# Scatters and gathers of 128 rows in place of 125, the last three to and from spare slots

## The chip, the cores and the metric

The kernel runs on one core of one Trainium2 chip. The metric is the device time of one execution in microseconds; its median of three runs is 7850.16 us. Engines are called by their names, and by the profile's short ones: TensorE (PE, with weight loads as PEld), VectorE (DVE), ScalarE (ACT), GpSimd (POOL), SyncE (SP). All of them issue work in program order and meet at semaphores. SyncE's DMAs go through queue 1, GpSimd's indirect ones through queue 0.

## The reference

Two layers of a graph transformer over 6250 nodes with 256 features. Only the last step of the second layer is touched: a mixture of eight experts, two for each node.

```python
x = x + _L1_ffn_ref(_layernorm(x), gate_w, gate_b, W1, b1, W2, b2)

# _L1_ffn_ref: N = 6250 rows, D = 256, H = 512, E = 8
logits = xf @ gate_w + gate_b
probs = softmax(logits)
top2_vals, top2_idx = top_k(probs, 2)
cw = zeros(N, E).at[rows, top2_idx].add(top2_vals)
for w1, bb1, w2, bb2, we in experts:
    h = gelu(xf @ w1 + bb1)
    out += we[:, None] * (h @ w2 + bb2)
```

## The kernel before

The 6250 rows stand in SBUF as NT = 50 tiles of P = 125 rows (`m.x`, 125 partitions x 50 x 256). `sorts_and_rows` sorts the edges and makes the rows' projections for the first layer, in an order of its engines' work that is written out once (`early_plan`, `weave`) and followed by each engine alone. Attention, slice attention and the relational layer follow, both graph layers with loops of indirect gathers of 128 rows (L1142 and L2055). The function `experts` comes last.

`experts` works in four steps.

1. *Gate.* ScalarE writes the normalized rows to `xn`, the first 125 partitions of the SBUF tensor `space` (128 x 50 x 256). TensorE turns each pair of tiles (L2760), VectorE copies the turned pair to SBUF (L2640), TensorE multiplies by the gate's weights (L2749), and VectorE and ScalarE make softmax and ranks in groups of GT = 10 tiles. TensorE and VectorE both wait for the gate's weights and bias (`s_g`) before their first work. At the end VectorE writes `place` (L2683): for each row and each of its two experts the slot in the sorted list.
2. *Scatter.* GpSimd issues 100 indirect DMAs (L2586), one for each tile and each choice, of 125 rows of 1 KB each, from `xn` to the DRAM tensor `moe_in`. It has MC = 105 chunks of 128 slots; each expert's rows begin at a chunk.
3. *Chunks.* SyncE waits for all scatters, loads `b1` and then the chunks (L2539) into a ring within `space`; TensorE, VectorE and ScalarE make the two products and the gelu; SyncE stores each chunk to `moe_out` (L2543).
4. *Gather.* After all stores GpSimd issues 100 indirect DMAs (L2595) that fetch each row's two results into a ring of RING_G = 8 slots, VectorE adds them with their weights to `m.x` (L2731, L2734), and SyncE stores five tiles at a time to the output (L2546).

Slots of `moe_in` that no row takes must hold finite numbers. SyncE fills the whole tensor with ones at L344, early in `sorts_and_rows`; the row stores of L365 and L366 stand behind it in the queue, and VectorE's copy at L607 waits for those stores before it may write its two row buffers again.

Of the kernel before, what the change touches and what calls it, by code (L numbers as in the profile page):

```python
# [13 lines left out]
ALU = mybir.AluOpType  # L14
ACT = mybir.ActivationFunctionType
AX = mybir.AxisListType
F32 = mybir.dt.float32
BF16 = mybir.dt.bfloat16
I32 = mybir.dt.int32
# [3 lines left out]
N, C, E = 6250, 256, 200000  # L23
P = 125
NT = N // P
H, D = 8, 32
EC = E // P
LANES = 128
# [187 lines left out]
def sorts_and_rows(nc, m, a, row_i, node_f):  # L216

    with ExitStack() as ctx:
        sb, ps, sem = m.scope(nc, ctx)
# [10 lines left out]
        s_fill, s_node_t, s_src = sem("se_s_fill"), sem("se_s_node_t"), sem("se_s_src")  # L230
# [39 lines left out]
        xn = [eb(f"xn{u}", [P, C]) for u in range(2)]  # L270
# [49 lines left out]
        with m.block() as block:  # L320
            @block.sync
            def _(sp):
                def sort_work():
                    sp.dma_start(key_a[:, :], a["src"].rearrange("(p j) -> p j", p=P)).then_inc(s_load, 16)
                    sp.dma_start(key_b[:, :], a["dst"].rearrange("(p j) -> p j", p=P)).then_inc(s_load, 16)
                    sp.dma_start(key_c[:, :], a["edge_type_8"].rearrange("(p j) -> p j", p=P)).then_inc(s_load, 16)
                    sp.dma_start(w_ps[:, :, 0:C], a["L0_gnn_Wp"].rearrange("(c p) n -> p c n", p=128)).then_inc(s_wp, 16)
                    sp.dma_start(w_ps[:, :, C:2 * C], a["L0_gnn_Wskip"].rearrange("(c p) n -> p c n", p=128)).then_inc(s_wp, 16)
                    sp.dma_start(w_kv[:, :, 0:C], a["L0_mix_Wk"].rearrange("(c p) n -> p c n", p=128)).then_inc(s_wp, 16)
                    sp.dma_start(w_kv[:, :, C:2 * C], a["L0_mix_Wv"].rearrange("(c p) n -> p c n", p=128)).then_inc(s_wp, 16)  # L330
                    sp.dma_start(a_row[:, 0, :], a["L0_gnn_a_src"].rearrange("a h f -> a (h f)").broadcast_to((128, C))).then_inc(s_wp, 16)
                    sp.dma_start(a_row[:, 1, :], a["L0_gnn_a_trg"].rearrange("a h f -> a (h f)").broadcast_to((128, C))).then_inc(s_wp, 16)
                    sp.dma_start(skip_b[:, :], a["L0_gnn_bias"].rearrange("(o c) -> o c", o=1)).then_inc(s_wp, 16)
                    sp.dma_start(w_q[:, :, :], a["L0_mix_Wq"].rearrange("(c p) n -> p c n", p=128)).then_inc(s_wq, 16)
                    sp.dma_start(w_m[:, :, :], a["L0_mix_Wm"].rearrange("(c p) n -> p c n", p=128)).then_inc(s_wq, 16)
                    sp.wait_ge(s_prep, 1)
                    sp.dma_start(key_c[:, :], a["dst"].rearrange("(p j) -> p j", p=P)).then_inc(s_load, 16)
                    sp.dma_start(key_b[:, :], a["src"].rearrange("(p j) -> p j", p=P)).then_inc(s_load, 16)
                    sp.dma_start(m.x[:, :, :], a["x"].rearrange("(t p) c -> p t c", p=P)).then_inc(s_x, 16)
                    for k in range(2 * COUNTED):  # L340
                        yield
                    sp.wait_ge(s_src, 1)
                    sp.dma_start(m.src_keys, keys[0][:, :]).then_inc(s_kept, 16)
                    sp.dma_start(m.moe_in.rearrange("(p a) (h c) -> p (a h) c", p=LANES, h=2),  # L344
                                 m.ones[:, :].unsqueeze(1).broadcast_to((128, 2 * MC, 128))).then_inc(s_fill, 16)
                    for k in range(SORTED):
                        yield

# [26 lines left out]
                sp.wait_ge(s_node_t, 1)  # L375
                sp.dma_start(m.node_t.rearrange("(p e) -> p e", p=128), keys[0][:, FS // 2:FS].bitcast(BF16)).then_inc(s_fill, 16)
                sp.wait_ge(s_kept, 16)
                sp.wait_ge(s_fill, 32)

            @block.vector  # L380
            def _(dve):
# [2069 lines left out]
GT = 10  # L2451
MC = (2 * N + NE * (LANES - 1)) // LANES
# [4 lines left out]
BACK_AT = HID_AT + 4  # L2457
RING_G = (NT - BACK_AT) // 2


def experts(nc, m, a, out):


    with ExitStack() as ctx:
        sb, ps, sem = m.scope(nc, ctx)
# [5 lines left out]
        space = sb("ex_space", [128, NT, C], F32)  # L2471
        xn = space[0:P, :, :]
        xs, ys = space[:, 0:RX, :], space[:, RX:RX + RY, :]
        b1 = space[:, BIAS_AT:HID_AT, :].rearrange("p (e h) c -> p e (h c)", h=2)
        hid = [space[:, HID_AT + 2 * u:HID_AT + 2 * u + 2, :].rearrange("p h c -> p (h c)") for u in range(2)]
        back = space[0:P, BACK_AT:BACK_AT + 2 * RING_G, :].rearrange("p (r k) c -> p r k c", k=2)
        xt = [sb(f"ex_xt{u}", [128, 2, 2 * P], F32) for u in range(2)]
        prob = sb("ex_prob", [P, NT, NE], F32)
        rank = sb("ex_rank", [P, NT, NE], F32)
# [10 lines left out]
        num = [sb(f"ex_num{u}", [P, NE], F32) for u in range(2)]  # L2490
        num_i = sb("ex_num_i", [P, NE], I32)
        base = sb("ex_base", [P, NE], F32)
        place = sb("ex_place", [P, 2, NT], I32)
        cw = sb("ex_cw", [P, 2, NT], F32)
        chunk_f = sb("ex_chunk_f", [1, MC], F32)
        chunk_e = sb("ex_chunk_e", [1, MC], I16)
# [12 lines left out]
                                     "s_sel", "s_pre", "s_place", "s_scat"))  # L2509
        s_b1, s_tc, s_xtc, s_h, s_hid, s_gelu, s_u, s_ht, s_y, s_ys, s_fin, s_out = (sem("ex_" + x) for x in (  # L2510
            "s_b1", "s_tc", "s_xtc", "s_h", "s_hid", "s_gelu", "s_u", "s_ht", "s_y", "s_ys", "s_fin", "s_out"))
        s_xs = [sem(f"ex_s_xs{r}") for r in range(RX)]
        s_st = [sem(f"ex_s_st{r}") for r in range(RY)]
        s_back = [sem(f"ex_s_back{r}") for r in range(RING_G)]
# [8 lines left out]
        with m.block() as block:  # L2523
# [26 lines left out]
            @block.scalar  # L2550
            def _(act):
                def exps(g):
                    act.wait_ge(s_sub, g + 1)
                    act.activation(prob[:, GT * g:GT * g + GT, :], prob[:, GT * g:GT * g + GT, :], ACT.Exp).then_inc(s_exp, 1)

                for i in range(pairs):
                    for j in range(2):
                        n = 2 * i + j
                        ins = act.activation(xn[:, n, :], m.x[:, n, :], ACT.Identity, scale=m.rstd[:, n:n + 1],
                                             bias=m.nmr[:, n:n + 1])  # L2560
                    ins.then_inc(s_xn, 1)
                    if i >= 7 and (i - 7) % 5 == 0:
                        exps((i - 7) // 5)
                exps(NT // GT - 1)
                for c in range(-2, MC - 1):
                    if c + 1 >= 0:
                        act.wait_ge(s_u, c + 2)
                        if c >= 1:
                            act.wait_ge(s_y, c)
                        act.copy(ht[(c + 1) % 2].rearrange("p q n -> p (q n)"), p_u[(c + 1) % 2][:, :]).then_inc(s_ht, 1)  # L2570
                    if c + 2 < MC:
                        act.wait_ge(s_hid, c + 3)
                        act.activation(hid[c % 2], hid[c % 2], ACT.Gelu).then_inc(s_gelu, 1)

            @block.gpsimd
            def _(pool):
                pool.affine_select(out=before[:, :, :], in_=m.ones[0:P, 0:NE * NE].rearrange("p (e j) -> p e j", e=NE),
                                   compare_op=ALU.is_gt, fill=0.0, base=0, pattern=[[1, NE], [-1, NE]],
                                   channel_multiplier=0).then_inc(s_tri, 1)
                pool.affine_select(out=tri_f[:, :], in_=m.ones[0:P, 0:P], compare_op=ALU.is_gt, fill=0.0, base=0,  # L2580
                                   pattern=[[1, P]], channel_multiplier=-1).then_inc(s_tri, 1)
                pool.wait_ge(s_xn, pairs)
                pool.wait_ge(s_place, 1)
                for n in range(NT):
                    for k in range(2):
                        pool.indirect_dma_start(out=m.moe_in, out_offset=bass.IndirectOffsetOnAxis(ap=place[:, k, n:n + 1], axis=0),  # L2586
                                                in_=xn[:, n, :], in_offset=None).then_inc(s_scat, 16)
                for r in range(RY):
                    pool.wait_ge(s_st[r], 16 * ((MC - 1 - r) // RY + 1))
                for n in range(NT):  # L2590
                    r = n % RING_G
                    if n >= RING_G:
                        pool.wait_ge(s_fin, n - RING_G + 1)
                    for k in range(2):
                        pool.indirect_dma_start(out=back[:, r, k, :], out_offset=None, in_=m.moe_out,  # L2595
                                                in_offset=bass.IndirectOffsetOnAxis(ap=place[:, k, n:n + 1], axis=0)
# [3 lines left out]
            def _(dve):  # L2600
# [28 lines left out]
                    dve.drain()  # L2629
                    dve.tensor_reduce(rank[:, GT * g:GT * g + GT, :], over[:, :, :, :], AX.X, ALU.add)  # L2630

                dve.wait_ge(s_tri, 2)
                dve.wait_ge(s_g, 32)
                dve.tensor_copy(tri[:, :], tri_f[:, :])
                dve.memset(full[:, :], 1.0)
# [17 lines left out]
                at, k = 0, 1  # L2653
# [26 lines left out]
                for k in range(2):  # L2680
                    dve.tensor_reduce(cw[:, k, :], run[k][:, :, :], AX.X, ALU.add)
                dve.drain()
                dve.tensor_copy(place[:, :, :], cw[:, :, :]).then_inc(s_place, 1)  # L2683
                dve.tensor_tensor(chunk_ge[:, :, :], m.count_p[0:1, 0:MC].unsqueeze(2).broadcast_to((1, MC, NE)),
                                  num[1][0:1, :].unsqueeze(1).broadcast_to((1, MC, NE)), ALU.is_ge)
                dve.drain()
# [19 lines left out]
                for c in range(-3, MC):  # L2706
                    if 0 <= c + 2 < MC:
                        k = c + 2
# [19 lines left out]
                for n in range(NT):  # L2728
                    r = n % RING_G
                    dve.wait_ge(s_back[r], 32 * (n // RING_G + 1))  # L2730
                    dve.scalar_tensor_tensor(out=back[:, r, 0, :], in0=back[:, r, 0, :], scalar=cw[:, 0, n:n + 1], in1=m.x[:, n, :],  # L2731
                                             op0=ALU.mult, op1=ALU.add)
                    dve.drain()
                    dve.scalar_tensor_tensor(out=m.x[:, n, :], in0=back[:, r, 1, :], scalar=cw[:, 1, n:n + 1],  # L2734
                                             in1=back[:, r, 0, :], op0=ALU.mult, op1=ALU.add).then_inc(s_fin, 1)

            @block.tensor
            def _(pe):
# [84 lines left out]
def program(nc, a, out):  # L2823
    with ExitStack() as ctx:
# [32 lines left out]
        m.skip_rows = nc.dram_tensor("skip_rows", (N, C), F32).ap()  # L2857
        m.table1 = nc.dram_tensor("table1", (R * N, C), F32).ap()
        m.node_t = nc.dram_tensor("node_t", (FS * LANES,), BF16).ap()
        m.moe_in = nc.dram_tensor("moe_in", (MC * LANES, C), F32).ap()  # L2860
        m.moe_out = nc.dram_tensor("moe_out", (MC * LANES, C), F32).ap()
        constants(nc, m)
        m.x = m.sb("x", [P, NT, C], F32)
        m.mean = m.sb("mean", [P, NT], F32)
# [102 lines left out]
```

## Time before and how its profile is read

| | |
|---|---|
| median of 3 runs | 7850.16 us (7850.01 to 7862.31) |
| the profiled execution | 7849.75 us |
| its span on the core | 7848.0 us |
| busy TensorE / VectorE / GpSimd | 69% / 66% / 44% of the span |

Busy times are sums over the instructions of an engine. The kernel is a row of stages with different limits, so a share of the whole span says little about one stage: stretches of the span are read instead. For a DMA that GpSimd issues, the duration in the trace is the engine's own work on it; when the data has landed is a second time, from issue to landing. "Idle before" is the time in which an engine did nothing ahead of an instruction, with what ended it; "issue" stands for nothing that the profile shows. "PEclk" is the granted TensorE clock as a share of its full speed.

### The profile page before, as it was taken

The numbers are of one execution on the slowest core, as the hardware profiler recorded it, in microseconds if no ns is written. First come the engines' busy times: TensorE is split into PE (matmuls) and PEld (weight loads), VectorE is DVE, ScalarE is ACT, GpSimd is POOL, SyncE is SP. The second block draws the span as 40 slices with busy tenths as digits, with TensorE's granted clock in tenths as the row PEclk, the third lists the DMA queues.
The fourth block names the chain that finished last, engine by engine and source line by source line (L and its number), as shares of the span: only waits on it lengthen the run. The fifth ranks groups of instructions, "written<-read, shape, count | busy, mean of one in ns | idle before, by whom it ended". The sixth has DMA issues, their size and how long they took to land. (4 is left out here: it accounts for less than half of the span.)

```text
span 7848.0 us, 86538 instructions
## 1 busy us (share of the span) xinstructions
PE 5431.4 (69%) x24766; PEld 3747.1 (48%) x24766; DVE 5164.8 (66%) x11681; ACT 1874.3 (24%) x4564; POOL 3485.0 (44%) x3441
## 2 busy tenths in 40 slices
PE   5877774555555555517799788888899999951991
PEld 2446663333333443314464333433777778750661
DVE  6457767888888877774467566676666767660332
ACT  0333332222223333212224200000222222210220
POOL 0000004777777777710000355555666777716006
PEclk8998886777777777759999899999999999965995
DMA  4100003444455555530013322222333333332223
GB/s 143 45 27 1 1 1 95 124 124 124 124 126 128 128 131 129 136 60 3 6 68 132 117 75 73 72 75 77 87 94 94 98 97 97 97 70 83 64 63 107
DMA packets 310188, 665.87 MB, mean 85 GB/s; under 512 B 77974, under 2 KB 173964, under 8 KB 302717
## 3 DMA queue, kind: packets, MB, share of 16 engines
q0 software_dynamic: 180352, 455.22, 23.0%
q1 hardware_dynamic: 129383, 205.31, 7.6%
q8 instruction: 199, 3.26, 0.2%
q14 instruction: 254, 2.08, 0.1%
HBM read 546.52 MB, written 113.55 MB: 84 GB/s over the span
## 5 line engine op out<-in xcount | busy, mean ns | idle before, releaser
L2055 POOL DMA_INDIRECT ag_rows<-table,row_src x1612 | 1595.8, 990 | 1896.5 <-POOLq L2847 1023.5
L1142 POOL DMA_INDIRECT at_rows<-table,row_dst x1612 | 1645.5, 1021 | 491.3 <-issue 450.8
L1308 PE MATMUL at_p_a<-at_rows,at_hot 128*125 128x264 f32 x3224 | 1132.0, 509 | 1014.6 <-issue 972.1
L1308 PEld LDWEIGHTS at_p_a<-at_rows,at_hot 128*125 128x125 f32 x3224 | 706.0, 245 | 1201.7 <-issue 1062.5
L2422 PE MATMUL mo_p_e<-ag_rows,ag_hot 128*125 128x256 f32 x2192 | 650.9, 422 | 293.9 <-DVE acc L2263 257.2
L1271 DVE TENSOR_TENSOR acc<-acc,at_p_a 125x264 f32 x1612 | 687.1, 426 | 245.0 <-PE at_p_a L1308 101.8
L2263 DVE TENSOR_TENSOR acc<-acc,mo_p_e 125x256 f32 x1096 | 459.0, 419 | 442.9 <-PE mo_p_e L2422 243.1
L2422 PEld LDWEIGHTS mo_p_e<-ag_rows,ag_hot 128*125 128x125 f32 x2192 | 391.5, 199 | 503.1 <-DVE acc L2263 394.8
L2165 DVE TENSOR_TENSOR mo_prod<-mo_far,mo_twice 125x256 f32<-125x256 f32 x1600 | 580.4, 419 | 51.6 <-issue 45.1
L1094 POOL PARTITION_ALL_REDUCE sb_top<-sb_top x1 | 0.4, 398 | 1220.8 <-DVE sb_top L1065 1220.8
L1258 DVE TENSOR_TENSOR at_rows<-at_rows 128x1024 f32<-128x1024 f32 x496 | 496.2, 1021 | 21.9 <-ACT at_rows L1190 21.6
L2127 ACT COPY qa_part<-mo_p_n 128x500 f32<-128x500 f32 x450 | 259.2, 576 | 737.6 <-PE mo_p_n L2306 735.1
L2286 PEld LDWEIGHTS mo_p_n<-m_near,qa_part 128*125 128x125 f32 x3200 | 399.1, 195 | 3.0
L1190 ACT ACTIVATE at_rows<-at_diff 128x104 f32<-128x104 f32 x124 | 35.8, 289 | 1526.4 <-DVE at_diff L1251 1526.4
L2286 PE MATMUL mo_p_n<-m_near,qa_part 128*125 128x33 f32 x3200 | 396.6, 269 | 0.0
L1921 PE MATMUL rt_p_w<-table_w,rt_xt 128*125 128x512 f32 x800 | 353.0, 594 | 0.0
L2595 POOL DMA_INDIRECT ex_space<-moe_out,ex_place x100 | 121.4, 1214 | 492.5 <-DMA moe_out<-ex_space 462.3
L2249 DVE TENSOR_TENSOR ag_hot<-count_p,node_src 128x500 f32<-128x500 f32 x403 | 272.4, 676 | 80.1 <-issue 80.0
L2263 DVE TENSOR_TENSOR acc<-acc,mo_p_m 125x256 f32 x516 | 215.6, 418 | 145.5 <-PE mo_p_m L2422 58.0
L2422 PE MATMUL mo_p_m<-ag_rows,ag_hot 128*125 128x256 f32 x1032 | 294.4, 410 | 23.4 <-DVE acc L2263 23.0
L1202 DVE TENSOR_TENSOR at_hot<-count_p,node_dst 128x500 f32<-128x500 f32 x496 | 290.3, 587 | 0.3 <-PEq L1060 0.3
L2286 PE MATMUL mo_p_n<-mo_prod,mo_v 125*33 125x512 f32 x800 | 280.4, 665 | 1.9 <-DVE mo_far L2165 1.9
(491 smaller groups left out, 9751.8 us busy)
## 6 DMA issues: line engine op xcount, KB each, us to landing
at_wide<-node_t SPq DMA_DIRECT2D x124, 406.2 KB
table<-rt_row SPq DMA_DIRECT2D x50, 1000.0 KB
at_rows<-table,row_dst POOLq DMA_INDIRECT x1612
ag_rows<-table,row_src POOLq DMA_INDIRECT x1612
moe_in<-ones SPq DMA_DIRECT2D x1, 13440.0 KB
ex_space<-moe_in SPq DMA_DIRECT2D x105, 128.0 KB, 2.2
moe_out<-ex_space SPq DMA_DIRECT2D x105, 128.0 KB, 1.7
table<-row SPq DMA_DIRECT2D x50, 128.9 KB
```

Of the source, the lines that this page charges most:

```text
L1142: pool.indirect_dma_start(out=rows[n % 3][:, g, :], out_offset=None, in_=m.table0, in_offset=bass.IndirectOffsetOnAxis(ap=row_i[:, n * G + ...
L1202: dve.tensor_tensor(hot[v][:, gs[0]:gs[0] + k, :], m.count_p[:, :].unsqueeze(1).broadcast_to((128, k, P)), node_f[:, bass.ds(n * G + gs[0] ...
L1258: dve.tensor_tensor(part[:, :, 0:C].rearrange("p g (h f) -> p g h f", h=H), part[:, :, 0:C].rearrange("p g (h f) -> p g h f", h=H), part[: ...
L1271: dve.tensor_tensor(row, row, p_a[(n * G + g) % BANKS][0:P, 0:TW], ALU.add).then_inc(s_acc, 1)
L1308: pe.matmul(p_a[k % BANKS][0:P, 0:TW], hot[n % 2][:, g, :], rows[n % 3][:, g, :], start=True, stop=True).then_inc(s_agg, 1)
L1921: mm = pe.matmul(p_w[k][0:P, :], xt[n % 2][:, c, :], w[:, c, 2 * k:2 * k + 2, :].rearrange("p r o -> p (r o)"), start=c == 0, stop=c == 1)
L2055: pool.indirect_dma_start(out=rows[:, i % RING, j, :], out_offset=None, in_=m.table1, in_offset=bass.IndirectOffsetOnAxis(ap=row_i[:, 2 * ...
L2165: return dve.tensor_tensor(out, far[u][:, 1, :, :], twice[:, :, s:s + D], ALU.mult)
L2249: dve.tensor_tensor(hot[n % 2][:, :, :], m.count_p[:, :].unsqueeze(1).broadcast_to((128, HOTS, P)), node_f[:, n * HOTS:n * HOTS + HOTS].un ...
L2263: dve.tensor_tensor(row, row, p_edge[bank[i]][0:P, C * j:C * j + C], ALU.add).then_inc(s_acc, 1)
L2286: add = lambda out, l, r: pe.matmul(out, l, r, start=False, stop=False, skip_group_check=True)
L2422: mm = pe.matmul(p_edge[bank[i]][0:P, C * j:C * j + C], hot[i // 2 % 2][:, 2 * (i % 2) + j, :], rows[:, i % RING, j, :], start=True, stop= ...
```

## The change

All 128 partitions of `space` are scattered, and 128 are gathered. For the three lanes 125 to 127 `place` holds numbers of slots behind the last chunk, another one for each lane, tile and choice, made by an iota on GpSimd. `moe_in` and `moe_out` grow by three chunks for them. Of `moe_out`, these three chunks are filled with ones by a second DMA behind the first fill. VectorE zeroes partitions 96 to 127 of `space` in five pieces, one for each group of ten tiles, ahead of its other work in `experts`, and ScalarE waits for each piece before it writes that group's rows. The first 125 lanes are handled as before.

```diff
@@ sorts_and_rows, SyncE
-                    sp.dma_start(m.moe_in.rearrange("(p a) (h c) -> p (a h) c", p=LANES, h=2),
+                    sp.dma_start(m.moe_in[0:MC * LANES, :].rearrange("(p a) (h c) -> p (a h) c", p=LANES, h=2),
                                  m.ones[:, :].unsqueeze(1).broadcast_to((128, 2 * MC, 128))).then_inc(s_fill, 16)
+                    sp.dma_start(m.moe_out[MC * LANES:, :].rearrange("(p a) (h c) -> p (a h) c", p=LANES, h=2),
+                                 m.ones[:, :].unsqueeze(1).broadcast_to((128, 6, 128))).then_inc(s_fill, 16)
...
-                sp.wait_ge(s_fill, 32)
+                sp.wait_ge(s_fill, 48)
@@ experts, tensors
-        back = space[0:P, BACK_AT:BACK_AT + 2 * RING_G, :].rearrange("p (r k) c -> p r k c", k=2)
+        back = space[:, BACK_AT:BACK_AT + 2 * RING_G, :].rearrange("p (r k) c -> p r k c", k=2)
-        place = sb("ex_place", [P, 2, NT], I32)
+        place = sb("ex_place", [128, 2, NT], I32)
+        s_clear = sem("ex_s_clear")
@@ experts, ScalarE
                         n = 2 * i + j
+                        if n % GT == 0:
+                            act.wait_ge(s_clear, n // GT + 1)
                         ins = act.activation(xn[:, n, :], m.x[:, n, :], ACT.Identity, scale=m.rstd[:, n:n + 1],
@@ experts, GpSimd
+                pool.iota(place[:, :, :], [[3 * NT, 2], [3, NT]], base=MC * LANES - P, channel_multiplier=1).then_inc(s_tri, 1)
                 pool.wait_ge(s_xn, pairs)
                 pool.wait_ge(s_place, 1)
...
                         pool.indirect_dma_start(out=m.moe_in, out_offset=bass.IndirectOffsetOnAxis(ap=place[:, k, n:n + 1], axis=0),
-                                                in_=xn[:, n, :], in_offset=None).then_inc(s_scat, 16)
+                                                in_=space[:, n, :], in_offset=None).then_inc(s_scat, 16)
@@ experts, VectorE
-                dve.wait_ge(s_tri, 2)
+                for g in range(NT // GT):
+                    dve.memset(space[96:128, GT * g:GT * g + GT, :], 0.0).then_inc(s_clear, 1)
+                dve.wait_ge(s_tri, 3)
...
-                dve.tensor_copy(place[:, :, :], cw[:, :, :]).then_inc(s_place, 1)
+                dve.tensor_copy(place[0:P, :, :], cw[:, :, :]).then_inc(s_place, 1)
...
-                    dve.scalar_tensor_tensor(out=back[:, r, 0, :], in0=back[:, r, 0, :], scalar=cw[:, 0, n:n + 1], in1=m.x[:, n, :],
+                    dve.scalar_tensor_tensor(out=back[0:P, r, 0, :], in0=back[0:P, r, 0, :], scalar=cw[:, 0, n:n + 1], in1=m.x[:, n, :],
@@ program
-        m.moe_in = nc.dram_tensor("moe_in", (MC * LANES, C), F32).ap()
-        m.moe_out = nc.dram_tensor("moe_out", (MC * LANES, C), F32).ap()
+        m.moe_in = nc.dram_tensor("moe_in", ((MC + 3) * LANES, C), F32).ap()
+        m.moe_out = nc.dram_tensor("moe_out", ((MC + 3) * LANES, C), F32).ap()
```

## Rows read from the trace of the kernel before

**Rows 1.** The page's chain of work that ended last, by line.
```profile
PE ex_p_h L2784 2%; PE ex_p_y L2802 2%; POOL moe_in L2586 2%; POOL ex_space L2595 1%; PE ex_p_g L2793 1%; PE ex_p_g L2749 0%; PE ex_p_t L2775 0%; PE ex_p_t L2760 0%; DMA ex_space<-moe_out,ex_place 0%; DMA ex_space<-moe_in 0%; DVE ex_xt L2640 0%; DVE ex_same L2622 0%; DVE ex_over L2628 0%; DVE ex_same L2625 0%; DVE ex_xtc L2704 0%
```
**Rows 2.** Busy time by stretch: length, busy PE, PEld, DVE, ACT, POOL, PEclk, DMA share, GB/s.
```profile
6984.00:6992.00 8.00, 8.00 (x42) 8.00 (x41) 2.16 (x4) 0.08 (x1) 0.00 (x0) 0.50 1.07 374
...
7066.00:7227.00 161.00, 0.00 (x0) 0.00 (x0) 4.57 (x9) 0.00 (x0) 118.98 (x100) 0.50 0.30 82
7685.00:7841.00 156.00, 0.00 (x0) 0.00 (x0) 48.01 (x100) 0.00 (x0) 121.39 (x100) 0.50 0.44 120
```
**Rows 3.** `moe_out`: ns min/median/max, starts; who waited (us, times).
```profile
L2595 POOL DMA_INDIRECT ex_space<-moe_out,ex_place x100: 1183/1202/1452, 7685.3 to 7835.6; - x100
...
  DVE ex_space L2731: 106.1, 41
```
**Rows 4.** Instructions of `moe_in`: the same columns.
```profile
L2586 POOL DMA_INDIRECT moe_in<-ex_space,ex_place x100: 1177/1182/1847, 7067.5 to 7221.8; - x100
```
**Rows 5.** Groups by line in both stretches: busy us, mean ns, idle before by releaser.
```profile
L2586 POOL DMA_INDIRECT moe_in<-ex_space,ex_place x100 | 119.0, 1190 | 128.6 <-DVE ex_place L2683 92.1 <-issue 36.6
...
L2595 POOL DMA_INDIRECT ex_space<-moe_out,ex_place x100 | 121.4, 1214 | 492.5 <-DMA moe_out<-ex_space 462.3 <-issue 29.9 <-DVE x L2734 0.3
```
**Rows 6.** The lines L1142 and L2055, and L1142's group on the page.
```profile
L1142 POOL DMA_INDIRECT at_rows<-table,row_dst x1612: 942/949/2010, 1247.6 to 3383.3; - x180
...
L2055 POOL DMA_INDIRECT ag_rows<-table,row_src x1612: 943/949/7527, 4437.5 to 6905.3; - x180
...
L1142 POOL DMA_INDIRECT at_rows<-table,row_dst x1612 | 1645.5, 1021 | 491.3 <-issue 450.8
```
**Rows 7.** DMA of 7100 to 7200 us (scatters), then of 6700 to 6800 (L2055).
```profile
DMA packets 8057, 8.13 MB, mean 81 GB/s; under 512 B 5855, under 2 KB 6170, under 8 KB 8056
q0 software_dynamic: 8056, 8.12, 29.8%
moe_in<-ex_space,ex_place POOLq DMA_INDIRECT x64, 3.7
...
DMA packets 3609, 9.95 MB, mean 99 GB/s; under 512 B 1200, under 2 KB 1200, under 8 KB 3600
ag_rows<-table,row_src POOLq DMA_INDIRECT x75
```
**Rows 8.** VectorE's two largest memsets of 4-byte numbers, by form.
```profile
L1063 DVE MEMSET acc<- 125x13200 f32 x1 | 11.1, 11058 | 4.2 <-issue 4.2
L389 DVE MEMSET keys<- 128x2048 f32 x2 | 3.5, 1765 | 0.9 <-issue 0.9
```
**Rows 9.** Timeline of the start of `experts`: start us, us, engine, line.
```profile
6974.81 6.50 ACT L2559 ACTIVATE ex_space<-x,nmr,rstd 125x256 f32<-125x256 f32 x13 [1.30 <-PEq L2931]
...
6978.81 0.23 DVE L2634 CAST ex_tri<-ex_tri_f 125x125 bf16<-125x125 f32 x1 [4.29 <-DMA ex_b_g<-in_L_ffn_gate_b]
6979.02 0.16 DVE L2635 MEMSET ex_full<- 125x125 bf16 x1
6979.89 0.68 DVE L2640 COPY ex_xt<-ex_p_t 128x500 f32<-128x500 f32 x1 [0.71 <-PE ex_p_t L2760]
```
**Rows 10.** Waits of 140 to 400 us, a stretch, and SyncE's row store behind the fill.
```profile
DVE row L607 <- DMA skip_rows<-skip: 18.4, 1, 18.4
...
147.00:200.00 53.00, 18.27 (x56) 8.55 (x56) 31.38 (x73) 8.00 (x19) 0.00 (x0) 0.69 1.02 296
...
177.97 20.89 SPq L365 DMA_DIRECT2D table<-row  x1
```
**Rows 11.** Timeline of SyncE's queue at the end: the last output store.
```profile
7840.77 0.27 SPq L2546 DMA_DIRECT2D out_x<-x  x1
```
**Rows 12.** DMA of 7700 to 7800 us: queues (packets, MB, share) and issues.
```profile
q0 software_dynamic: 8334, 8.40, 33.1%
q1 hardware_dynamic: 4128, 4.20, 13.3%
...
ex_space<-moe_out,ex_place POOLq DMA_INDIRECT x67, 4.2
```

More of the change, by code:

```diff
@@ L2730, in _ @@
                     dve.wait_ge(s_back[r], 32 * (n // RING_G + 1))
-                    dve.scalar_tensor_tensor(out=back[:, r, 0, :], in0=back[:, r, 0, :], scalar=cw[:, 0, n:n + 1], in1=m.x[:, n, :],
+                    dve.scalar_tensor_tensor(out=back[0:P, r, 0, :], in0=back[0:P, r, 0, :], scalar=cw[:, 0, n:n + 1], in1=m.x[:, n, :],
                                              op0=ALU.mult, op1=ALU.add)
                     dve.drain()
-                    dve.scalar_tensor_tensor(out=m.x[:, n, :], in0=back[:, r, 1, :], scalar=cw[:, 1, n:n + 1],
-                                             in1=back[:, r, 0, :], op0=ALU.mult, op1=ALU.add).then_inc(s_fin, 1)
+                    dve.scalar_tensor_tensor(out=m.x[:, n, :], in0=back[0:P, r, 1, :], scalar=cw[:, 1, n:n + 1],
+                                             in1=back[0:P, r, 0, :], op0=ALU.mult, op1=ALU.add).then_inc(s_fin, 1)
             @block.tensor
```

## The prediction

> **What bounds the kernel now.** The change lives in the last stage, experts, so I read that stage and not the shares of the span. First the chain that ended last: two of its costliest entries are single GpSimd lines, the scatter (L2586) and the gather (L2595) [rows 1]. Then busy time by stretch [rows 2]: in 7066 to 7227 us and in 7685 to 7841 us TensorE does nothing and GpSimd is busy 119 of 161 and 121 of 156 us. Nobody else has work there that could cover it: the chunks can't be read before every row is scattered, and VectorE in the gather stage is busy 48 us, waiting 106 us for gathered rows [rows 3]. So in both stretches the time is that of 100 indirect DMAs issued one after the other. One scatter costs 1190 ns in the mean and 0.30 us of gap; 99 intervals from 7067.5 to 7221.8 us are 154.3 us, which is 99 x 1.49 = 147.5 plus a few longer gaps (36.6 us of "issue" in 99 gaps). One gather costs 1214 ns and the same gap; from 7685.3 to 7835.6 us are 150.3 us = 99 x 1.518 [rows 3 to 5]. Between them lie the chunks, bound by TensorE, which the change doesn't touch.
>
> **What an indirect DMA of 128 rows costs.** The kernel holds 3224 of them. L2055 gathers 128 rows of the same 1 KB as a scatter or gather here: median 949 ns, minimum 943; L1142, with rows of 1056 bytes, has the same 949 [rows 6]. The scatters of 125 rows have a median of 1182 and a minimum of 1177, the gathers 1202 and 1183. That the smaller DMA takes longer is the fact on which all rests, so I looked for a second sign of it in the packets [rows 7]. Of 125 rows, 64 DMAs made 8056 packets, 126 each: 1886/64 = 29.5 of 2 to 8 KB, (6170-5855)/64 = 4.9 of 0.5 to 2 KB, and 91.5 small ones. Of 128 rows, 75 DMAs made the 3600 under 8 KB, 48 each, and 1200 of these are small: 32 of 2 to 8 KB (four rows each) and 16 small ones. The 125 rows are thus cut like five shares of 25 rows (six packets of four rows, one of a single row), the 128 rows like 16 shares of 8. More than twice the packets, 0.23 us more on GpSimd. I can't see in the trace which part of GpSimd's work makes the 0.23 us, but direction and table don't: scatter and gather of 125 rows agree within 20 ns, the two gathers of 128 exactly.
>
> The Trainium skill says of this (DMA: Bandwidth & Descriptors, Why a DMA increments its semaphore by 16 and not by 1) that a DMA uses the largest number of engines up to 16 that divides its outermost sizes, so 5 for 125 and 16 for 128; the packets agree, and it states no price on GpSimd. Another section (Anatomy of one DMA, SWDGE path) speaks against the change: a fixed 2.0 us plus bytes, with descriptor generation small; by it 3 KB more are an estimated 7 ns more each, 1.4 us in all, and the sum below would be a loss of some 9 us. The rows, 949 against 1182 ns, speak against that reading; the mechanism stays as rival A.
>
> **The sum.** Terms, each with both ends:
> - *Scatters*: no 128-row scatter exists. VectorE is nearly idle there. Today the mean is 8 ns over the median, so 949 + 8 = 957 ns; 100 x (1190 - 957) = 23.3 us less. Ends: the minimum 943 and the mean of all L1142, 1021 (VectorE busy beside it): 24.7 and 16.9.
> - *Gathers*: mean 12 ns over the median today and the median 20 over the scatters'; I carry both: 949 + 32 = 981 ns; 23.3 us less. Ends 943 and 1021: 27.1 and 19.3.
> - *The gap* of 0.30 us stands behind DMAs of either size, so it stays.
> - *Landing after the last one*: a scatter lands in 3.7 us, a gather in 4.2 (median). In 7100 to 7200 us queue 0 took 29.8% of 16 engines for 64 x 125 rows: 477 / 8000 = 60 ns per row and engine. A share of 25 rows is 1.5 us, one of 8 is 0.5. So 1.0 us less twice at most; at the last gather an output store is in the way, so I take 1.5 together (0 to 2.0).
> - *Clearing lanes 96 to 127*: five memsets of 2560 columns stand ahead of VectorE's first work in experts. Fewer partitions needn't be cheaper, so I go by columns: 2048 took 1765 ns, 13200 took 11058, so 0.833 ns a column and 2560 are 2.19 us; five are 10.95 us [rows 8], some 0.1 less if they overlap like cast and small memset (0.02 us). Today VectorE idles 4.29 us until the gate bias lands at 6978.81, casts, sets one tile, and copies the first turned tile at 6979.89 [rows 9]. The block starts near 6974.8 (ScalarE's first work), so the memsets last to 6985.65; cast and small memset take 0.37 us, and the copy starts near 6986.0: 6.1 us late (5.5 to 6.5). TensorE's gate matmuls wait for this copy, and afterwards TensorE is busy 8.00 of 8 us, at the granted clock 0.50, the lower of its two levels [rows 2]; nothing takes the delay up, and the placement and the scatters come 6.1 us later. ScalarE now waits for the first memset, 2.2 us: its first pair is then ready near 6978.1, before the bias at 6978.81, for which TensorE waits too; free. It would be late only if a memset took over 2.8 us. Its later waits are passed by then. GpSimd's one iota hides under the memsets.
> - *The second fill*: 384 rows, 0.39 MB, behind 13440 KB on SyncE's queue. From 147 to 200 us the DMA engines are full (share 1.02, 296 GB/s), SyncE sticks 20.89 us at the first row store and VectorE 18.4 us at L607 for a skip store's landing [rows 10]; VectorE, ScalarE and TensorE follow one written order there, so I let the delay pass whole to the end of that stage. 0.39 MB / 296 GB/s = 1.3 us; with its issue 1.5 us (0 to 3.0).
> - *The rest* (SyncE's wait for 48 in place of 32 long after landing, wider views) is nothing; the cover is the sort stage, and uncovered the fill is the same 1.3 us.
>
> Sum: -23.3 - 23.3 - 1.5 + 6.1 + 1.5 = -40.5. The profiled execution took 7849.75 us (span 7848.0 and 1.75 around it), within a microsecond of the median of 7850.16, so the forecast is **7809 us**. All good ends give -24.7 - 27.1 - 2.0 + 5.5 = -48.3, 7801; all bad ones -16.9 - 19.3 + 6.5 + 3.0 = -26.7, 7823. That is the own range of the likeliest.
>
> **Rivals.**
> - *A, the price goes with rows and bytes.* Then 949 belongs to the earlier stages' form, and 128 rows cost 128/125 of today's: 1219 and 1243 ns, +2.9 and +2.9, with +6.1 and +1.5: +13.4, **7863**, slower. It decides from a mean over 1202 - 38 = 1164 ns per DMA, where 200 DMAs no longer pay the 7.6 us of clears and fill. For it: no 128-row DMA stands in this stage. Against it: rows of different tables and stages with one price per size, and the packets.
> - *B, the output stores hold up the gathers.* Ten stores of 625 rows run beside them. The last, issued at 7840.77, ends the span at 7848.0: 7.2 us [rows 11]. Queue 1 had 4128 packets at 13.3% of 16 engines: 213 / 4128 = 52 ns each; 625 rows on 5 engines are 6.5 us, on 16 only 2.0, so stores seem to sit on few engines [rows 12]. A gather that must use all 16 then always meets them. Load of such an engine per five tiles: 6.5 + 10 x 8 x 63 ns (queue 0 at 33.1% for 67 gathers) = 11.5 us, against 12.8 us of issuing and 15.2 today. It fits with 10% to spare, and the ring of eight slots covers some 20 us. If it doesn't, the gather stage keeps its 150 us: -40.5 + 23.3 = -17.2, **7833**.
> - *C, only gathers have the price of 949*, scatters keep theirs, +2.9: -40.5 + 23.3 + 2.9 = -14.3, **7835**.
>
> **How the numbers follow.** The forecast gets 0.80, A 0.06, B 0.06, C 0.05; 0.03 is left for what I haven't seen. The range from 7800 to 7834 takes in the likeliest's bounds and B. A difference of 0.2% (15.7 us) is about what a measurement of this kernel can tell from none; the bound lies at 7834.5. Faster: 0.80 + 0.06 and a little of the rest = 0.87. Same: C and most of A, which at 13 us is under the bound, 0.10. Slower: 0.03.
>
> **What the profile after should show.** Scatters near 957 ns, gathers near 981, the gap still 0.30; both stretches some 23 us shorter; 48 packets per DMA; five memsets near 2.19 us and the first gate copy 6.1 us later after the stage's start; VectorE's wait at L607 longer by 1 to 2 us; SyncE's stores no later against VectorE's last row. What would make it wrong: a duration over 1.1 us at 128 rows, gaps that grow above 0.30 where GpSimd waits for VectorE (a full ring), or clears that cost 2x their price.

## The result, and the profile after

The changed kernel takes 7802.85 us in the median of six runs (7790.52 to 7812.09), the kernel before 7851.36 in six (7849.85 to 7862.31). The ratio is 0.9934, 95% interval 0.9922 to 0.9947: 0.66% faster, clear of the 0.2% bound. On the first median, 7850.16, that is 7798 us: the forecast of 7809 had the direction, but was 11 us short, and the range ended at 7800. The profiled execution took 7803.55 us, span 7801.8, 46.2 us less than before.

The two kinds of DMA first: the lines of `moe_in` and `moe_out`, then the group of the scatters in the stretch of the scatter stage.

```profile
L2592 POOL DMA_INDIRECT moe_in<-ex_space,ex_place x100: 959/963/1771, 7076.9 to 7203.4; - x100
...
L2601 POOL DMA_INDIRECT ex_space<-moe_out,ex_place x100: 945/949/1201, 7665.1 to 7790.7; - x100
```

```profile
L2592 POOL DMA_INDIRECT moe_in<-ex_space,ex_place x100 | 97.3, 973 | 120.5 <-DVE ex_place L2691 90.3 <-issue 30.2
```

Beside [rows 3 to 5]: a scatter's median went from 1182 to 963 ns, a gather's from 1202 to 949, and the gathers' minimum is L2055's 943 within 2 ns. The 99 intervals are 126.5 us for the scatters (154.3 before) and 125.6 for the gathers (150.3). There is one more change, in the last number of the scatters' group: 30.2 us of "issue" in 99 gaps where there were 36.6, now the plain 0.30 us each.

Packets and landing, from the DMA view of 7100 to 7200 us (scatters) and of 7680 to 7780 us (gathers with stores), to be read beside [rows 7, 12]:

```profile
q0 software_dynamic: 3781, 10.31, 25.5%
...
moe_in<-ex_space,ex_place POOLq DMA_INDIRECT x80, 2.4
```

```profile
q0 software_dynamic: 3769, 10.32, 34.3%
q1 hardware_dynamic: 5040, 5.12, 15.2%
...
ex_space<-moe_out,ex_place POOLq DMA_INDIRECT x79, 3.7
```

A scatter lands in 2.4 us in place of 3.7. The packets are best counted over the whole stage, where no DMA is cut at the ends of the stretch: queue 0 has 4800 for the 100 scatters of 128 rows (7076 to 7212 us) and 12800 for those of 125 (7067 to 7232 us of the trace before), so 48 and 128 a DMA. My 126 was a little low. Now the start of experts, a timeline:

```profile
6975.83 0.31 POOL L2585 TENSOR_SCALAR_AFFINE_SELECT ex_tri_f<-ones 125x125 f32<-125x125 f32 x1
...
6976.15 2.19 DVE L2639 MEMSET ex_space<- 32x2560 f32 x1 [0.86 <-PEq L2939]
...
6978.83 2.19 DVE L2639 MEMSET ex_space<- 32x2560 f32 x1 [0.48 <-issue]
...
6986.43 0.21 POOL L2587 IOTA ex_place<- 128x100 int32 x1 [10.29 <-issue]
6986.85 2.19 DVE L2639 MEMSET ex_space<- 32x2560 f32 x1 [0.48 <-issue]
6989.07 0.23 DVE L2642 CAST ex_tri<-ex_tri_f 125x125 bf16<-125x125 f32 x1
...
6989.35 1.20 DVE L2648 COPY ex_xt<-ex_p_t 128x500 f32<-128x500 f32 x2
```

A memset costs the 2.19 us that I had worked out, to the digit, but 0.48 us of idle stand ahead of each of the last four (0.86 ahead of the first). The stage starts at 6975.55 (SyncE's load of the gate's weights; 6974.78 before), so the first copy is 13.8 us into it, against 5.1 before: 8.7 us later, not 6.1. GpSimd's iota waits 10.29 us for nothing that the profile shows; here the memsets hide it. It comes back below.

The difference by stretch, from the first starts of these lines in both traces (us, worked out from starts that are printed to 0.1, so a value can be off by 0.1; the first three places are SyncE's fill L344, the first gather L1142 and the first gather L2055, which is L2057 in the changed kernel):

| stretch | before | after | difference |
|---|---|---|---|
| start of the span to the fill | 147.7 | 141.1 | -6.6 |
| fill to the first gather L1142 | 1099.9 | 1099.1 | -0.8 |
| to the first gather L2055 | 3189.9 | 3191.2 | +1.3 |
| to experts | 2537.3 | 2544.1 | +6.9 |
| experts to the first scatter | 92.7 | 101.4 | +8.7 |
| 99 scatters | 154.3 | 126.5 | -27.8 |
| last scatter to the first chunk load | 4.1 | 2.8 | -1.3 |
| chunks | 459.4 | 458.9 | -0.5 |
| 99 gathers | 150.3 | 125.6 | -24.7 |
| last gather to the end | 12.4 | 11.1 | -1.3 |

The stage of experts gives 47 us; the rest is 0.8 the other way, but only because -6.6 and +6.9 meet there. Whether these two belong to the change is what the next runs had to tell.

### The profile page after: what moved, and what is told of

It reads as the page before. It is cut to its first block and busy times, and to the rows that moved or that the text cites. A ratio compares the mean times of both kernels' runs of the same rounds, so it can differ in the third digit from the quotient of the medians.

```text
span 7801.8 us, 86547 instructions
## 1 busy us (share of the span) xinstructions
PE 5445.0 (70%) x24766; PEld 3753.0 (48%) x24766; DVE 5174.9 (66%) x11686; ACT 1874.4 (24%) x4564; POOL 3440.3 (44%) x3442
## 5 line engine op out<-in xcount | busy, mean ns | idle before, releaser
L2057 POOL DMA_INDIRECT ag_rows<-table,row_src x1612 | 1596.6, 990 | 1901.7 <-POOLq L2855 1022.7
L2265 DVE TENSOR_TENSOR acc<-acc,mo_p_e 125x256 f32 x1096 | 458.9, 419 | 446.1 <-PE mo_p_e L2424 245.9
L1260 DVE TENSOR_TENSOR at_rows<-at_rows 128x1024 f32<-128x1024 f32 x496 | 496.0, 1020 | 22.0 <-ACT at_rows L1192 21.7
L2601 POOL DMA_INDIRECT ex_space<-moe_out,ex_place x100 | 96.5, 965 | 490.8 <-DMA moe_out<-ex_space 460.7
L2424 PE MATMUL mo_p_m<-ag_rows,ag_hot 128*125 128x256 f32 x1032 | 294.4, 410 | 23.3 <-DVE acc L2265 22.9
```

Of the source, the lines that this page charges most:

```text
L1260: dve.tensor_tensor(part[:, :, 0:C].rearrange("p g (h f) -> p g h f", h=H), part[:, :, 0:C].rearrange("p g (h f) -> p g h f", h=H), part[: ...
L2057: pool.indirect_dma_start(out=rows[:, i % RING, j, :], out_offset=None, in_=m.table1, in_offset=bass.IndirectOffsetOnAxis(ap=row_i[:, 2 * ...
L2265: dve.tensor_tensor(row, row, p_edge[bank[i]][0:P, C * j:C * j + C], ALU.add).then_inc(s_acc, 1)
L2424: mm = pe.matmul(p_edge[bank[i]][0:P, C * j:C * j + C], hot[i // 2 % 2][:, 2 * (i % 2) + j, :], rows[:, i % RING, j, :], start=True, stop= ...
```

## The experiments

**Both kernels again**, unchanged, five rounds. The second trace of each is what the places outside experts need.

> The kernel before once more, unchanged. Theory 1, the part of the gain beyond the terms of the sum is scatter between executions: ratio 1.000 with an interval that holds 1, but its trace differs from the first one by several us in places that nothing distinguishes, above all in the start (VectorE's first work at 9.28 us before, 2.45 us after) and in the relational stage (4437.5 to 6974.8 us before, some 7 us less than in the trace after). Theory 2, those differences belong to the change (code further along, other addresses): the trace repeats the start at 9.3 us and the length of the relational stage within 1 us. The two gaps of 3.5 us in the scatters (after the 40th and the 81st) should be there again at the same DMAs if they belong to the 125 rows or to the place in the code, and elsewhere or not at all if they are chance.

> The changed kernel once more, unchanged. Theory 1 (scatter between executions): the experts stage repeats the first trace within 2 us (first scatter 101.4 us after the stage's start, 99 intervals in 126.5 us, gathers 125.6 us, 11.1 us from the last gather to the end), while the time before the stage (6975.6 us in the first trace) may differ by up to 10 us. Ratio between 0.993 and 0.995. Theory 2 (the change also speeds what stands ahead of experts): the start repeats at 2.5 us and experts starts within 1 us of 6975.6.

Ratios 0.9994 (0.9980 to 1.0007) and 0.9941 (0.9923 to 0.9958), on another chip, where the kernel before takes 8328.68 us, 6% more. In the traces of the kernel before it is 488 us; 259 of them lie in the stretch with the attention loop, 229 in the relational stage, and none in experts. Inside experts both repeat: 92.7 and 101.4 us to the first scatter, 154.3 and 126.1 us of scatters, 149.6 and 125.7 us of gathers, and the two long gaps are at the same scatters (ahead of number 39 and 78, counted from 0; the places that I named in the expectation were miscounted). From the first gather L2055 to experts the stretch took 2766.6 us in one and 2750.1 in the other; over the eight traces on chips of 7850 us it lies between 2527 and 2554 us with no order by kernel (2537.2 and 2537.3 without the change's code, 2537.3, 2544.1 and 2553.7 among those with it). So the +6.9 us is scatter. The start is not: 147.4 us again before, 141.8 again after. Theory 2 holds for it, theory 1 for the rest.

**What GpSimd pays for**, by one kernel with ten sizes.

> The changed kernel with another number of lanes in each group of five tiles, for scatters and gathers alike: 128, 125, 120, 112, 96, 64, 126, 124, 127, 125. It leaves out the lanes above that number, so it scatters and sums only part of the rows; its time is of no use, only the duration of each group's ten DMAs. Theory 1, what GpSimd pays for is the number of shares that divide the rows (16 for 128, 112, 96 and 64; 15 for 120; 14 for 126; 5 for 125; 4 for 124; 1 for 127): 128, 112, 96 and 64 cost 0.95 us or somewhat less with fewer rows, 120 and 126 near 1.0, 124 and 125 about 1.2, 127 over 1.2. Theory 2, only the full 128 rows are cheap and everything below has an added cost: all others near 1.18. Theory 3, price goes with the rows: 64 rows cost half of 128, and 127 and 126 no more than 128.

```diff
+SIZES = (128, 125, 120, 112, 96, 64, 126, 124, 127, 125)
...
-                                                in_=space[:, n, :], in_offset=None).then_inc(s_scat, 16)
+                                                in_=space[0:SIZES[n // 5], n, :], in_offset=None).then_inc(s_scat, 16)
```

(the offsets and the gathers' target are cut alike). Some rows of the timeline, scatters of 128, 125, 120, 112, 96, 64, 126, 124, 124 and 127 lanes in this order:

```profile
7567.51 0.96 POOL L2593 DMA_INDIRECT moe_in<-ex_space,ex_place  x1 [0.30 <-issue]
...
7581.28 1.18 POOL L2593 DMA_INDIRECT moe_in<-ex_space,ex_place  x1 [0.31 <-issue]
...
7595.15 0.99 POOL L2593 DMA_INDIRECT moe_in<-ex_space,ex_place  x1 [0.30 <-issue]
...
7607.81 0.94 POOL L2593 DMA_INDIRECT moe_in<-ex_space,ex_place  x1 [0.30 <-issue]
...
7622.49 0.91 POOL L2593 DMA_INDIRECT moe_in<-ex_space,ex_place  x1 [0.30 <-issue]
...
7636.97 0.89 POOL L2593 DMA_INDIRECT moe_in<-ex_space,ex_place  x1 [0.30 <-issue]
...
7647.16 0.98 POOL L2593 DMA_INDIRECT moe_in<-ex_space,ex_place  x1 [0.30 <-issue]
...
7662.32 1.31 POOL L2593 DMA_INDIRECT moe_in<-ex_space,ex_place  x1 [0.31 <-issue]
7668.14 1.31 POOL L2593 DMA_INDIRECT moe_in<-ex_space,ex_place  x1 [4.51 <-issue]
...
7700.03 2.54 POOL L2593 DMA_INDIRECT moe_in<-ex_space,ex_place  x1 [9.05 <-issue]
```

| lanes | shares x rows | scatter, median us | gather, median us |
|---|---|---|---|
| 64 | 16 x 4 | 0.90 | 0.90 |
| 96 | 16 x 6 | 0.91 | 0.91 |
| 112 | 16 x 7 | 0.935 | 0.92 |
| 128 | 16 x 8 | 0.96 | 0.95 |
| 120 | 15 x 8 | 0.99 | 0.98 |
| 126 | 14 x 9 | 0.98 | 0.99 |
| 125 | 5 x 25 | 1.18 | 1.21 |
| 124 | 4 x 31 | 1.31 | 1.28 |
| 127 | 1 x 127 | 2.54 | 2.54 |

(A share is what one DMA engine gets of the rows.) Theory 1 holds in every row, and the table says more than it did: in the main the price follows the rows of one share. 120 rows in 15 shares of 8 cost what 126 in 14 of 9 do; twice the rows at 16 shares (64 to 128) cost 0.06 us; from 31 to 127 rows a share it rises by 1.23 us, 12.8 ns a row. It isn't the whole price: 128 lanes cost 0.03 us less than 120 with as many rows a share. 126 lanes would have had nearly the whole gain, and 127 would have been a disaster. By the Trainium skill's rule (DMA: Bandwidth & Descriptors, Why a DMA increments its semaphore by 16 and not by 1) the share counts in the second column are what these row counts give. The order of the prices agrees with it, and so do the packets: the 100 scatters of this kernel made 12160 (queue 0, 7560 to 7732 us), exactly the sum if each share is cut into packets of up to four rows and each of the 16 engines gets as many packets as a share has, and one more (48 for 128, 112, 96 and 120 lanes, 32 for 64, 64 for 126, 128 for 125, 144 for 124, 528 for 127). The number of packets alone is not the price either: 96, 112 and 128 lanes have 48 and cost 0.91, 0.935 and 0.96 us. Theories 2 and 3 are out, and rival A with them. Which part of GpSimd's work takes the time no trace shows.

**One half at a time.**

> The changed kernel with its gathers back at 125 lanes; scatters of 128, clears and second fill stay. Nothing is left out. If the terms add: scatter stage 126.5 us as after, gathers back at 150 us, so about 25 to 26 us slower than the changed kernel: ratio to the kernel before about 0.9965 to 0.9975 (20 to 27 us faster). If my rival B held in part (output stores and gathers in each other's way) the gathers would already have differed; here they should repeat 1202 ns in the median.

> The changed kernel with its scatters back at 125 lanes; gathers of 128, clears and second fill stay. Nothing is left out. The scatter stage goes from 126.5 us to 147.5 if the two gaps of 3.5 us in the kernel before belonged to chance or code placement, to 154 if they belong to scatters of 125 rows. So 22 to 29 us slower than the changed kernel, ratio to the kernel before 0.996 to 0.998.

```diff
 # scatters_only (the offsets are cut alike)
-                        pool.indirect_dma_start(out=back[:, r, k, :], out_offset=None, in_=m.moe_out,
+                        pool.indirect_dma_start(out=back[0:P, r, k, :], out_offset=None, in_=m.moe_out,
...
 # gathers_only (the offsets are cut alike)
-                                                in_=space[:, n, :], in_offset=None).then_inc(s_scat, 16)
+                                                in_=space[0:P, n, :], in_offset=None).then_inc(s_scat, 16)
```

Each is 0.9965 of the kernel before (0.9953 to 0.9977 and 0.9952 to 0.9978), inside what was expected. The stage times are those of the parts: scatters 126.2 and gathers 150.7 us in the first, 155.0 and 125.9 in the second (126.5 and 125.6 with both, 154.3 and 150.3 before). With 125 lanes the two long gaps are there again, here the first of them:

```profile
7115.07 1.18 POOL L2592 DMA_INDIRECT moe_in<-ex_space,ex_place  x1 [0.30 <-issue]
7119.77 1.19 POOL L2592 DMA_INDIRECT moe_in<-ex_space,ex_place  x1 [3.52 <-issue]
```

**Whose are the gaps?** In all four traces in which every scatter has 125 lanes (both of the kernel before, this one, and one below) GpSimd stands 3.5 us ahead of scatter 39 and of scatter 78, counted from 0; in the six in which all have 128 lanes never.

> The changed kernel with 128 lanes in the first 50 scatters and 125 in the last 50. Nothing is left out. In four traces with 125 lanes in all scatters GpSimd stood 3.5 us ahead of the scatters number 39 and 78 (counted from 0), in four with 128 lanes never. Theory 1: scatters of 125 fill something up, 39 of them; then the one gap is at number 89. Theory 2: the gaps belong to the place in the program, and 128 lanes only hide them; then there is one at 78. Theory 3: it takes a longer row of 125s than 50: no gap.

```diff
+                        L = 128 if n < 25 else P
...
-                                                in_=space[:, n, :], in_offset=None).then_inc(s_scat, 16)
+                                                in_=space[0:L, n, :], in_offset=None).then_inc(s_scat, 16)
```

```profile
7170.05 1.18 POOL L2593 DMA_INDIRECT moe_in<-ex_space,ex_place  x1 [0.30 <-issue]
7175.25 1.17 POOL L2593 DMA_INDIRECT moe_in<-ex_space,ex_place  x1 [4.02 <-issue]
```

One gap of 4.02 us, ahead of scatter number 72: none of the three. It isn't the place in the program (78), and not 39 scatters of 125 alone (89). The gap comes as if something filled that scatters of both sizes add to, those of 125 some three times as much: 39 of them, or 50 of 128 and 22 of 125, so one of 128 counts like 17/50 = 0.34 of one of 125. The packets (48 to 128, 0.375) are near that ratio and not equal to it: by packets the gap would have come at number 70 or 71. In the kernel of ten sizes gaps stand at numbers 78 (4.51 us, 124 lanes) and 87 (9.05 us, 127 lanes, the last row of its fence), also at the sizes with the largest shares.

One count fits all of these places. Let each scatter add the rows of one of its shares, and one: 26 for 125 lanes, 9 for 128. Ahead of the first gap the sums are then 39 x 26 = 1014 with 125 lanes throughout, 50 x 9 + 22 x 26 = 1022 in the mixed kernel, and 996 in that of ten sizes (740 for its first seven, and 8 x 32 for 124 lanes); one more scatter makes each of them 1028 or more. Ahead of the second gap they are 78 x 26 = 2028 and, with ten sizes, 740 + 10 x 32 + 7 x 128 = 1956, and one more makes 2054 and 2084: about twice the first. A hundred scatters of 128 lanes add up to 900 and meet neither. This count was fitted after the runs and none was made to test it, and the gathers don't follow it: 100 of 125 lanes had no such gap in four traces. So what fills isn't settled; that the 6.4 us belong to 125 lanes and not to a place in the program is.

**The clears moved to GpSimd.**

> The changed kernel with the five clears of lanes 96 to 127 issued by GpSimd in place of VectorE; nothing is left out. If the 8.7 us by which the first gate copy is late come from VectorE's queue alone, they go almost whole: first scatter some 93 to 95 us after the stage's start, against 101.4, and the kernel 7 to 8 us faster than the changed one (ratio about 0.992 to 0.993 against the kernel before). The rival: ScalarE then waits for GpSimd's slower memsets; if one of 2560 columns takes over 5 us, the pace of ScalarE's groups of ten tiles, the gate stage is late by the excess and most of the gain is gone.

```diff
@@ experts, VectorE
-                for g in range(NT // GT):
-                    dve.memset(space[96:128, GT * g:GT * g + GT, :], 0.0).then_inc(s_clear, 1)
-                dve.wait_ge(s_tri, 3)
+                dve.wait_ge(s_tri, 2)
@@ experts, GpSimd
+                pool.wait_ge(s_tri, 2)
+                for g in range(NT // GT):
+                    pool.memset(space[96:128, GT * g:GT * g + GT, :], 0.0).then_inc(s_clear, 1)
+                pool.wait_ge(s_clear, NT // GT)
                 pool.iota(place[:, :, :], ...
@@ experts, VectorE, before it writes the places
+                dve.wait_ge(s_tri, 3)
                 dve.tensor_copy(place[0:P, :, :], cw[:, :, :]).then_inc(s_place, 1)
```

Its group by line, and the start of its stage, which begins at 7430.68:

```profile
L2589 POOL MEMSET ex_space<- 32x2560 f32 x5 | 11.0, 2244 | 0.1
```

```profile
7433.58 7.97 ACT L2564 ACTIVATE ex_space<-x,nmr,rstd 125x256 f32<-125x256 f32 x16 [4.18 <-POOL ex_space L2589]
...
7435.92 0.68 DVE L2650 COPY ex_xt<-ex_p_t 128x500 f32<-128x500 f32 x1
```

GpSimd clears 2560 columns in 2.2 us as VectorE does, without gaps, so the rival's slow memset isn't there. The first copy is 5.2 us into the stage (13.8 in the changed kernel, 5.1 in the one before), the first scatter 92.6: the whole 8.7 us are back. Ratio to the kernel before 0.9928 (0.9910 to 0.9945), beside 0.9941 for the changed kernel on that chip. The ratios' intervals overlap, so the two times alone don't show the 8.7 us; the stage times do.

**The start.** Two of GpSimd's first instructions and SyncE's first load in the kernel before, a timeline, then the same in the changed one:

```profile
1.07 0.20 POOL L92 MEMSET ones<- 3x128 bf16 x1
8.40 0.25 POOL L93 IOTA count_p<- 128x125 f32 x1 [7.14 <-issue]
...
11.46 0.39 SPq L324 DMA_DIRECT2D key_a<-in_src  x1
```

```profile
1.07 0.20 POOL L92 MEMSET ones<- 3x128 bf16 x1
1.57 0.25 POOL L93 IOTA count_p<- 128x125 f32 x1 [0.31 <-issue]
...
4.62 0.39 SPq L324 DMA_DIRECT2D key_a<-in_src  x1
```

The whole gain of 6.6 us is here: SyncE's first load (L324) starts at 11.46 us before and at 4.62 after, 6.8 us earlier like the iota that stands ahead of it, and the fill keeps 6.6. The change does nothing at this place, but it puts an iota near the end of the kernel.

> The kernel before with one thing of the change: an iota on GpSimd behind its two selects at the start of experts, written to a spare tensor that nobody reads. Everything is computed. Theory 1: the 6.9 to 7.1 us that GpSimd stands before its first iota of the kernel (0.3 us in all traces of kernels made from the changed one) is a load that the experts' iota leaves ready for the next execution; then the start is short here too: first iota at 1.6 us in place of 8.2 to 8.4, the fill issued near 141 us in place of 147.5, and a kernel 6 to 7 us faster (ratio 0.9991 to 0.9992, hardly to be told from 1). Theory 2: it belongs to something else of the change (longer program, wider tensors); then the start stays at 8.2 to 8.4 us. In both the experts stage shows a wait of 8 to 10 us before the iota, hidden behind the gate.

> The changed kernel with the iota of the places ahead of the two selects. Nothing is left out. Theory 1 in its narrow form: what GpSimd has last run before the end decides; with a select last, as in the kernel before, the first iota of the kernel starts at 8.2 to 8.4 us. If any iota in experts is enough, it starts at 1.6 us as in the changed kernel.

```diff
 # iota_only, on the kernel before
+        spare = sb("ex_spare", [128, 2, NT], I32)
...
+                pool.iota(spare[:, :, :], [[3 * NT, 2], [3, NT]], base=0, channel_multiplier=1)
                 pool.wait_ge(s_xn, pairs)
 # iota_first, on the changed kernel: the line of the iota is moved ahead of GpSimd's two selects
```

The kernel with the iota alone:

```profile
1.58 0.24 POOL L93 IOTA count_p<- 128x125 f32 x1 [0.31 <-issue]
...
L2583 POOL IOTA ex_spare<- 128x100 int32 x1 | 0.2, 215 | 10.9 <-issue 10.9
```

The start is the short one, 1.58 us, and the fill is issued at 141.6; in experts the iota stands 10.9 us, which nobody waits for. With the iota ahead of the selects it is the same, 1.57 us. So one late iota, whose result nobody reads, makes the program's first iota start some 6.8 us earlier, and the late one needn't be GpSimd's last compute instruction. The late one runs 6966 us after the first, so I read this as something that one execution leaves ready for the next, perhaps the instruction's code; no trace shows two executions in a row, and the profile names no such thing. The ratio of the times, 0.9994 (0.9983 to 1.0004), can't tell 6 us from none.

**The output stores split**, on the kernel with the clears on GpSimd.

> The changed kernel with the clears on GpSimd, and each of the ten output stores of 125 lanes split into one of 120 and one of 5. Nothing is left out. If the store of 125 lanes is slow because it lies on few engines (52 ns a row, 25 rows for each of five: 6.5 us of the 7.2 us between its issue and the end), 120 lanes on more engines bring the time from the last issue to the end from 7.2 to 3 to 4.5 us, and the gathers, which meet the stores less, stay within 0.5 us of 125.7. So 3 to 4 us faster than the kernel with the clears on GpSimd, ratio about 0.991 to 0.993 against the kernel before. If the tail is the landing in DRAM whatever the shares, it stays at 7.2 us.

```diff
-                    sp.dma_start(out.rearrange("(t p) c -> p t c", p=P)[:, 5 * k:5 * k + 5, :],
-                                 m.x[:, 5 * k:5 * k + 5, :]).then_inc(s_out, 16)
-                sp.wait_ge(s_out, 16 * (NT // 5))
+                    for lo, hi in ((0, 120), (120, P)):
+                        sp.dma_start(out.rearrange("(t p) c -> p t c", p=P)[lo:hi, 5 * k:5 * k + 5, :],
+                                     m.x[lo:hi, 5 * k:5 * k + 5, :]).then_inc(s_out, 16)
+                sp.wait_ge(s_out, 32 * (NT // 5))
```

The last gather starts at 7765.3 and the span ends at 7774.7: 9.4 us in place of 11.1 in the changed kernel. The gathers take 125.3 us. Ratio 0.9917 (0.9903 to 0.9930): the lowest ratio here, 0.8% under the kernel before, though its interval overlaps that of the kernel with the clears on GpSimd (0.9928). The expectation missed: from the last issue (7769.4) to the end there remain 5.3 us, between the 3 to 4.5 of one theory and the 7.2 of the other, and the gain is 1.7 us of the 3 to 4 expected. Even shares explain a part of the tail; the rest is not explained.

## Why the prediction was right and wrong

- *The bound and the mechanism* were right: both stretches are GpSimd's alone, and 128 lanes cost there what they cost in the earlier loops.
- *Scatters*, durations: 23.3 us forecast, 21.7 measured (mean 973 ns, not 957). *Gathers*: 23.3 forecast; the intervals shrank by 24.7 (mean 965 ns, not 981).
- *The gap stays*: this is the first step that failed. I had noted "99 x 1.49 = 147.5 plus a few longer gaps (36.6 us)" and then let all gaps stand. The longer ones were two of 3.5 us that belong to scatters of 125 lanes; 6.4 us more gain.
- *Nothing changes ahead of the fill*: the second step that failed, and it wasn't written down as one. The sum had no term for the start, where the changed kernel gains 6.6 us through an iota of the execution before it. I had costed that iota at nothing, hidden under the memsets; there it does cost nothing.
- *Clears*: mechanism right and every us passed on, size off: 8.7 us in place of 6.1 (5.5 to 6.5). The row with which I priced the memset says "0.9 <-issue 0.9" for two [rows 8]; that is 0.45 us of idle ahead of each, near the 0.48 measured here, and I read only the duration. The block's first memset also came 0.6 us later than the 0.0 that I took.
- *Landing*: 1.5 forecast; the two stretches behind the last DMA shrank by 1.3 each, of which some 0.2 is the shorter last DMA itself. So about 1.0 twice, the "at most" of the forecast, and the store in the way took nothing off.
- *Second fill*: +1.5 forecast, and the traces can neither show nor exclude as much. From the fill to L1142 the time is 1099.9 and 1100.4 us in the kernel before, 1096.4 with the iota alone, and between 1098.0 and 1102.6 in the nine traces with the second fill. SyncE sticks at the new fill (49.99 us) in place of the row store, and VectorE's wait at L607 (now L609) is 18.2 us where it was 18.4.
- *Rival B* (stores against gathers): stores took 15.2% and gathers 34.3% of the engines and the gathers weren't held up: 0.30 us of gap each, as forecast. *Rivals A and C* fell with the first row of the profile.

Put together: -40.5 forecast; -6.6 (start), -6.4 (gaps), +1.6 (scatter durations), -1.4 (gathers), -1.1 (landing), -2.3 (fill), -0.5 (chunks) and +2.6 (clears) give -54.6. The ratio says 51.8 (42 to 61 by its interval). The two traces differ by 46.2: with the +6.9 and +1.3 us of the stages in between, which the sum leaves out as scatter, -54.6 is -46.4, and the last 0.2 is the last scatter, counted twice.

So what took the time out of the range are the two terms that I had put at nothing, the long gaps and the start, 13.0 us together. Without them the ratio's 51.8 would be 38.8, beside 40.5 forecast. That this is so near is in part luck: the clears and the scatters' durations were 4.2 us worse than forecast, the other terms 5.3 better.

## What to carry to other kernels

The price of an indirect DMA on GpSimd went here with the rows in one of its shares, not with its bytes: a row count with a large divisor up to 16 (128, 126, 120) was worth 0.2 us a DMA against 125, and 127 cost 1.6 us more than 128; pad the lanes, and give the padding a place of its own. Read the idle ahead of an instruction in the row from which its price is taken. Put new small work on the engine that waits in that stage: the same five clears cost 8.7 us on VectorE and nothing on GpSimd.

## What the runs showed of the hardware that was not expected

- GpSimd stood 6.9 and 7.1 us before its first iota in the two traces of the kernel before, whose last part has no iota, and 0.3 us in the ten traces with one there; that late iota waits instead (8.0 to 11.1 us in nine of them, not to be told apart in the tenth), where it can be hidden.
- Scatters of 125 lanes made GpSimd stand 3.5 us after each 39 of them, in four traces of four; gathers of 125 never did.
- Memsets of 2560 columns on VectorE stood 0.48 us apart, on GpSimd not at all, at equal duration (2.19 and 2.24 us).
- The kernel before took 7850 us on some chips and 8329 on another; the difference lay in the stages with gathers from large tables, and the experts stage was the same on both within 1.1 us.
